# Last group of a four-group transformer kernel: norms four and five, the feed-forward and the second attention's projections by halves of two batches

## What is computed

```
h = tok(x, ids)                          # embeddings, norm, gate
h = h + attn0(norm(h))                   # first attention, causal sums
h = h + ffn0(norm(h))                    # routed attention or mix, then:
#   n2 = norm(h') * g2 + b2
#   ffn = gelu(n2 @ W1 + bf1) @ W2 + bf2      192 -> 768 -> 192
h = h + attn1(norm(h))                   # 12 heads of 16: q, k, v, softmax, sum
h = h + experts(norm(h))                 # top 2 of 8 experts, 192 -> 768 -> 192
norm(x) = (x - mean) / sqrt(var + 1e-5)
```

## Time and profile before

| What | Before |
|---|---|
| Median of 3 runs | 883.57 us (882.9 to 883.79) |
| The profiled execution | 883.04 us, of it 881.2 us span |
| PE busy | 726.0 us (82%), 5500 records |
| DVE busy | 519.7 us (59%) |
| ACT busy | 301.4 us (34%) |
| POOL busy | 242.8 us (28%) |
| Chain that ended last | PE 59%, DVE 21%, issue 6%, ACT 5%, POOL 4%, DMA 3% |

### The profile page before, as it was taken

The page is one execution under the profiler, slowest core; times in us unless marked ns, Lnnn a source line. Parts: engine busy times, 40 slices in busy tenths (PEclk is TensorE's granted clock), DMA queues, the critical chain, the costliest instruction groups (busy, mean ns, idle before and its releaser), DMA issues.

```text
span 881.2 us, 15579 instructions
## 1 busy us (share of the span) xinstructions
PE 726.0 (82%) x5500; PEld 549.1 (62%) x5501; DVE 519.7 (59%) x1752; ACT 301.4 (34%) x688; POOL 242.8 (28%) x300
## 2 busy tenths in 40 slices
PE   0888777989678998868898977959767999999993
PEld 0546465566457565646666655745456988998892
DVE  7558757874678884668877466791344553333330
ACT  0033232624333263434244334313233423333330
POOL 5332200460013245001444200231001453333332
PEclk9999989999988999998899996798897999999997
DMA  7950000000000000000121000029001233222220
GB/s 248 412 244 2 0 1 1 19 8 1 1 1 32 24 19 7 1 2 1 37 37 8 1 2 2 5 94 361 27 1 28 42 73 46 36 37 38 36 35 8
DMA packets 29894, 43.63 MB, mean 50 GB/s; under 512 B 5355, under 2 KB 24597, under 8 KB 29830
## 3 DMA queue, kind: packets, MB, share of 16 engines
q1 hardware_dynamic: 19250, 30.87, 10.2%
q0 software_dynamic: 8752, 9.07, 6.4%
q10 hardware_dynamic: 1828, 2.84, 0.9%
HBM read 21.36 MB, written 22.09 MB: 49 GB/s over the span
## 4 chain that ended last, share of the span: by engine, by line
PE 59%; DVE 21%; issue 6%; ACT 5%; POOL 4%; DMA 3%; ACTq 1%; SPq 1%; DVEq 0%; POOLq 0%
PE qc L1829 26%; PE qa L1829 25%; PE qc L1832 4%; PE qa L1832 4%; DVE mx L1424 2%; DMA out<-qk_T 2%; DVE st L1036 1%; POOL arena_w L435 1%; DMA mu_row<-in_mu 1%; ACT big L791 1%; DVE qk_T L1430 1%; DVE arena_b L1376 1%; ACTq L627 1%; DVE arena_e L1250 1%; DVE xb L1053 1%
## 5 line engine op out<-in xcount | busy, mean ns | idle before, releaser
L1829 PE MATMUL qc<-arena_w,big 128*128 x468 | 82.8, 327 | 1.4 <-DVE qk_T L1808 1.4
L1829 PEld LDWEIGHTS qc<-arena_w,big 128*128 128x128 f32 x468 | 75.1, 190 | 2.1 <-issue 2.0
L1829 PE MATMUL qa<-arena_b 128*128 128x128 f32 (+2 forms) x688 | 73.6, 289 | 3.0 <-DVE att L1440 2.1
L1829 PEld LDWEIGHTS qa<-arena_b 128*128 128x128 f32 (+2 forms) x688 | 64.9, 192 | 11.7 <-issue 2.8
L1829 PE MATMUL qa<-arena_e,nT 128*128 128x192 f32 (+2 forms) x256 | 70.0, 430 | 1.1 <-DVE ga L1320 0.7
L1002 ACT ACTIVATE big<-qa,arena_b 128x128 f32<-128x128 f32 x156 | 43.0, 374 | 75.8 <-PE qc L1829 68.7
L597 POOL DMA_INDIRECT out<-qk_T x39 | 61.0, 1565 | 20.5 <-issue 10.5
L1797 DVE COPY arena_b<-qc 128x256 f32<-128x256 f32 x39 | 16.6, 426 | 84.1 <-PE qc L1832 84.1
L1829 PEld LDWEIGHTS qa<-arena_e,nT 128*128 128x128 f32 x256 | 47.4, 200 | 23.0 <-issue 12.9
L471 POOL TENSOR_TENSOR rs_a<-rs_a,minus_half 128x8 f32<-128x8 f32 x4 | 6.6, 1644 | 175.6 <-DVE rs_a L1287 175.6
L475 POOL TENSOR_TENSOR rs_b<-rs_b,minus_half 128x4 f32<-128x4 f32 x12 | 12.5, 1041 | 152.2 <-DVE rs_b L1049 152.2
(11 more groups left out here) (366 smaller groups left out, 1576.5 us busy)
## 6 DMA issues: line engine op xcount, KB each, us to landing
slots<-xk SPq DMA_DIRECT2D x1, 13192.0 KB, 43.1
arena_e<-in_w SPq DMA_DIRECT2D x8, 579.0 KB, 7.7
arena_w<-in_w SPq DMA_DIRECT2D x8, 576.0 KB, 9.4
qk_T<-slots SPq DMA_DIRECT2D x39, 97.0 KB, 1.9
out<-hb SPq DMA_DIRECT2D x16, 96.0 KB
arena_e<-in_w_l SPq DMA_DIRECT2D x1, 804.0 KB
arena_e<-in_W ACTq DMA_DIRECT2D x1, 768.0 KB
out<-qk_T POOLq DMA_INDIRECT x39, 3.5
```

What stands on the lines that cost most here:

```text
L1829: return nc.tensor.matmul(o, l, r, start=start, stop=stop)
```

## The change

It touches the last group alone; the joint stages keep their code.

- ln4: the statistics, the small operations and the root are made for batches 0 and 1, then for batches 2 and 3 (`half_stats`, `half_apply`, `root_half`). The last group's second `selected_in` moves behind the first half's statistics on DVE.
- Feed-forward: each of the 6 up products becomes two products of 256 tokens; those of the first half wait for the first half of `xT` only. The 6 blocks lie in six banks (PD, PA, PB) instead of taking turns in four. `down_half` waits for the gelus of its own half.
- ln5 by halves in the same way, the first half ahead of `ffn_out` of the second.
- q and k products by halves of 256 tokens in six banks (PA, PB, PC), `v1_half` for two batches behind each half.
- ACT's and POOL's lists follow the same order.

```
+            def root_half(name, n, hf):
+                w(NG - 1, name, n)
+                pool.tensor_tensor(rs_b[:, 1, 2 * hf:2 * hf + 2], rs_b[:, 0, 2 * hf:2 * hf + 2], minus_half[:, 0:2], ALU.pow)\
+                    .then_inc(s["rstd_b"], 1)
...
             def back(tb):
-                root_back(tb, "ln4")
+                root_half("ln4", 9, 0)
+                root_half("ln4", 18, 1)
                 residual(tb, 0)
                 residual(tb, 1)
                 residual(tb, 2)
                 residual(tb, 3)
-                root_back(tb, "ln5")
-                root_back(tb, "ln6")
+                root_half("ln5", 9, 0)
+                root_half("ln5", 20, 1)
+                root_last()
...
+            def gelu_half(tb, j, hf):
+                w(tb, "up", FJ * hf + j + 1)
+                A(hid[:, j, two(hf)], (PD, PA, PB)[j // 2][:, j % 2, two(hf)], ACT.Gelu, bias=bf1c[:, j:j + 1])\
+                    .then_inc(*done("gelu"))
+
+            def qk1_evac_half(tb, n, hf):
+                w(tb, "qk1", 6 * hf + n + 1)
+                A(q1k1[:, n % 2, n // 2, two(hf)], (PA, PB, PC)[n // 2][:, n % 2, two(hf)], ACT.Copy).then_inc(*done("qk1_e"))
...
                 n4T_evac(tb, 0)
                 n4T_evac(tb, 1)
-                ffn_gelu(tb, 0)
...
+                for hf in range(2):
+                    for j in range(FJ):
+                        gelu_half(tb, j, hf)
                 x5T_evac(tb, 0)
+                qk1_evac_half(tb, 0, 0)
+                qk1_evac_half(tb, 1, 0)
+                qk1_evac_half(tb, 2, 0)
+                qk1_evac_half(tb, 3, 0)
                 x5T_evac(tb, 1)
...
+                qk1_evac_half(tb, 4, 0)
+                qk1_evac_half(tb, 5, 0)
                 v1_evac(tb, 0)
+                for n in range(6):
+                    qk1_evac_half(tb, n, 1)
                 v1_evac(tb, 1)
...
             def back(tb):
-                ln4_stats(tb)
-                ln4_apply(tb)
+                ln4_half(tb, 0)
+                selected_in(tb, 1)
+                ln4_half(tb, 1)
+                ln4_half_apply(tb, 0)
+                ln4_half_apply(tb, 1)
                 ffn_out(tb, 0)
+                ln5_half(tb, 0)
+                ln5_half_apply(tb, 0)
                 ffn_out(tb, 1)
-                ln5_stats(tb)
-                ln5_apply(tb)
+                ln5_half(tb, 1)
+                ln5_half_apply(tb, 1)
...
+            def up_half(tb, j, hf):
+                w(tb, "n2T", hf + 1)
+                if j == 4:
+                    w(tb, "hin", 2 * G)
+                if hf:
+                    w(tb, "gelu", j + 1)
+                inc(both((PD, PA, PB)[j // 2][:, j % 2, two(hf)], lambda k: w_up[:, k, j * 128:(j + 1) * 128],
+                         lambda k: xT[:, k, two(hf)]), "up")
+
+            def down_half(tb, b):
+                w(tb, "gelu", FJ * (b // 2 + 1))
...
+            def qk1_half(tb, n, hf):
+                w(tb, "x5T_e", hf + 1)
+                if hf:
+                    w(tb, "qk1_e", n + 1)
+                elif n >= 4:
+                    w(tb, "h_ffn", 2 * (n - 3))
...
             def logits(tb, b, wide=False):
                 lag = 2 if wide else 1
                 if b == 0:
-                    w(tb, "qk1_e", 6)
+                    w(tb, "qk1_e", 12 if wide else 6)
                     w(tb, "v1", 2)
```

More of the change, by code:

```diff
@@ L330, in tok, with two @@
             return slice(b * 128, b * 128 + 128)
+        def two(hf):
+            return slice(hf * 256, hf * 256 + 256)
         def bc(ap, axis, n):
@@ L1449, in ln6_apply @@
                 dve.wait_ge(s["keep"], AHEAD + tb * PER["keep"])
-                dve.wait_ge(s["rstd_b"], root_b(tb, 2) + 1)
+                dve.wait_ge(s["rstd_b"], root_b(tb, 2) + (3 if tb == NG - 1 else 1))
                 norm_apply("ln6", hb, x6, rs_b, mv_b)
@@ L2037, in n4_T @@
                 for b in (2 * hf, 2 * hf + 1):
-                    w(tb, "ln4", 11 + b + 1)
+                    w(tb, "ln4", (18 if tb == NG - 1 else 11) + b + 1)
                     for c in range(C):
@@ L2054, in ffn_down, with v1_half @@
                 inc(i, "down")
+            def up_half(tb, j, hf):
[8 more added lines that the diff above has]
+                w(tb, "gelu", FJ * (b // 2 + 1))
+                for j in range(FJ):
+                    i = mm(psl(PC, b, D), hid[:, j, tok(b)], w_down[:, j, :], j == 0, j == FJ - 1)
+                inc(i, "down")
+            def qk1_half(tb, n, hf):
[4 more added lines that the diff above has]
+                    w(tb, "h_ffn", 2 * (n - 3))
+                j, wt = n // 2, (w_1q, w_1k)[n % 2]
+                inc(both((PA, PB, PC)[j][:, n % 2, two(hf)], lambda k: wt[:, k, 4 * j:4 * j + 4, :].rearrange("p h d -> p (h d)"),
+                         lambda k: xT[:, k, two(hf)]), "qk1")
+            def v1_half(tb, hf):
+                w(tb, "x5T_e", hf + 1)
+                for b in (2 * hf, 2 * hf + 1):
+                    inc(both(psl(PD, b, H * (HD + 1)), lambda c: xT[:, c, tok(b)],
+                             lambda c: w_1v[:, c, :, :].rearrange("p h d -> p (h d)")), "v1p")
             def x5_T(tb, hf):
                 for b in (2 * hf, 2 * hf + 1):
-                    w(tb, "ln5", 11 + b + 1)
+                    w(tb, "ln5", (9 + b + 1 if hf == 0 else 18 + b + 1) if tb == NG - 1 else 11 + b + 1)
                     for c in range(C):
@@ L2346, in back @@
                 n4_T(tb, 0)
+                up_half(tb, 0, 0)
+                up_half(tb, 1, 0)
                 n4_T(tb, 1)
[L2348 to L2356, removed]
-                ffn_down(tb, 3)
+                up_half(tb, 2, 0)
+                up_half(tb, 3, 0)
+                up_half(tb, 4, 0)
+                up_half(tb, 5, 0)
+                for j in range(FJ):
+                    up_half(tb, j, 1)
+                for b in range(G):
+                    down_half(tb, b)
                 x5_T(tb, 0)
+                qk1_half(tb, 0, 0)
+                qk1_half(tb, 1, 0)
+                qk1_half(tb, 2, 0)
+                qk1_half(tb, 3, 0)
                 x5_T(tb, 1)
-                qk1(tb, 0)
-                qk1(tb, 1)
-                qk1(tb, 2)
-                qk1(tb, 3)
-                qk1(tb, 4)
-                qk1(tb, 5)
-                v1_rows(tb, 0)
-                v1_rows(tb, 1)
+                qk1_half(tb, 4, 0)
+                qk1_half(tb, 5, 0)
+                v1_half(tb, 0)
+                for n in range(6):
+                    qk1_half(tb, n, 1)
+                v1_half(tb, 1)
                 logits(tb, 0, True)
```

50 lines of the change are left out of this document (38 added, 12 removed).

## The result

The change takes the kernel to 879.12 us (median of 6 runs, 870.22 to 880.45); the kernel before, run beside it, takes 882.82 (881.65 to 883.79). The ratio is 0.9944, 95% interval 0.9917 to 0.9971: faster by 3.7 us, 3 us short of the forecast of 876.0 and inside its range. That fall is where to look: the stages that the change touches did slightly better than forecast, and something behind them got slower.

The account below looks back on a forecast made before the run. Bound: one chain through the last group's back stage, where PE's waits for ln4 and ln5 also slow its clock. Gains 1.2 + 6.4 = 7.6 took the profiled 883.04 to 875.4, median 876.0 us; range 873.0 to 879.5.

Parts of the forecast that it names:

- First part, ln4 and up: ln4 to down products: halves start the up products 1.65 us earlier, partly lost to slow clock; gain 1.2 (1.0 to 1.8).
- lock rule: Named with a first part of 1.0 and a late first half for the upper 877.5; not defined in the text given.
- The up phase's other waits: Up phase: last-gelu wait of 0.76 us goes, first gelu has 1 us of slack, POOL's later residuals cost nothing.
- Second part, ln5 and q, k, v: Down products to first logits: first half's norm hidden, 8.05 against 8.08 us; 15.9 instead of 22.3, gain 6.4.
- Half-width records: Up, q and k products: 0.22 us per 256-column record, bounds 0.217 and 0.23; 48 records take 10.56 us.
- The rival of narrow products that pay for their loads: The 96 new records: loads not hidden, 0.38 us each, 15.4 more, 891.4 us; chance 0.03.
- What comes behind: After the logits: expert weights land at about 619, over 20 us cover their reader, and the gain reaches the end.
- the clock is less kind: Attention or pause before q and k: more slow clock costs 3 us, 879.0; one slow stretch alone 877.5; chance 0.18.
- a chance to gain: Slow stretch from 667.03 to 677.28, around the first expert products: at full clock 2.9 us saved, 873.1; chance 0.14.
- The prediction's own sign of being wrong: Behind the changed stages: the logits come early, at about 634.3, and the expert tiles do not.

Follow-up runs that it names:

- ln4 filled: Changed kernel with eight unread products in attention gaps, plus five more while PE waits for ln4: 869.55 us, ratio 0.9838 to the kernel before.
- the four profiles: Changed kernel unchanged (879.12 and 886.5 us), with four unread products ahead of the first logits (880.67), and with two behind them (884.63).
- the shift: Changed kernel with four unread products ahead of the last group's first logits, putting its attention off: 880.67 us.
- the filled kernels: Changed kernel and kernel before, each with eight unread products in the last group's attention gaps: 878.27 against 889.96 us, then 878.18 against 889.94.
- the changed kernel with two fillers: Changed kernel with only two unread 512-column products, behind the first batch's logits: 884.63 us, ratio 0.989 to the kernel before.
- the second set: Later runs together: changed kernel unchanged 886.5 us, kernel before 893.4, both with eight unread products 878.18 and 889.94, changed with two 884.63.

## Why the prediction was right in its place and short in its size

**First part, ln4 and up: right, more than taken.** Predicted were up products 7.2 us behind the selected rows, down products 13.0 to 13.8 behind the up products, and a gain of 1.2 (1.0 to 1.8). Measured: 6.49, 13.87, gain 2.36 - 0.70 = 1.66. Three terms made the start earlier. The half chains were shorter: from the first half's rows to the second's (590.87) it is 1.93 us, not 2.12, and both variances are done 3.96 behind the start, not 4.24. Most of that is the selected rows, 0.53 for a pair and not 0.68; the seven small operations take 0.84 on two columns where they took 0.86 on four. The root takes 0.70 to 0.76, not 1.02. And the first applies were not slowed: 0.66 for two beside the root, at the lower end of the two values the step kept open. The pair began before the second root (592.98, 0.76 long) and ended while it ran, the second apply inside it, at undisturbed length (0.67 at ln5 with POOL idle). The prediction's upper value of 877.5 takes in a "lock rule": no run shows such a term, and what the runs showed in its place are these 0.66 us with the root running beside them. Beside POOL's additions the next pair did double (1.31), as the earlier trace rows had shown. The other half of the step was right as well: the earlier start cost more slow clock, 2.8 us of it (13.87 against 11.1), and with ln4 filled the phase takes 10.90, so that there was no more to get in it.

**The up phase's other waits: right.** No wait for the last gelu, none for the first, whose table is loaded by 602.41: the first two gelus end at 603.27, and PE comes to the second half's first block at 604.12; the residuals end at 598.6 and delay nobody.

**Second part, ln5 and q, k, v: right.** The first half's normed rows are ready 7.62 us behind the first down product (predicted 8.05 of 8.08): the narrow root took 0.71, and sum, statistics and small operations took less than their 2.10. The cover was 7.80 us and not 8.08 (the transposes start at 617.10), so 0.2 us were left, and PE did not wait. q follows 1.12 behind the down products (1.2), the clock stays at 1.00, and the second half's transposes run at 621.94, 1.1 us after their rows are ready (0.8). From the last down product to the logits 15.64 (15.9). Gain 6.75, predicted 6.4.

**Half-width records: right.** Sixteen of them take 3.45 us in the chain, 0.216 each, at the lower bound of 0.217. The rival of narrow products that pay for their loads is out.

**What comes behind: right for transfers and experts, wrong for the attention.** The weights have landed by about 620, and windows over the expert loop show PE as full as before (19.80 of 20.00 at 720 to 740). The term that failed is in the rival "the clock is less kind": "a second and third of these, with 3.08 busy each, cost at most 1.5 each", with a price of 3 and a chance of 0.18, and against it "PE's own pattern stays". I had read the 3.42 us of the earlier trace rows as the length of a slow stretch. It was the length of one, and the second line of the same rows showed another of 10.25 us, with 2.98 of its first 3.42 busy, which I took for a chance to gain and not for a warning. At a granted clock of 0.50 this attention keeps PE busy for 2.2 to 2.9 us of each 3.4 up to its last wait, and in none of the four profiles did the clock return before the expert products. ("Busy half of the time" was low as well: it is 17.95 of 30.40 us, 0.59.)

The price of that case was 6.05 us in the profile (8.07 more of PE's busy time, 2 of it in gaps), double the 3 taken, and by times and clocks it was the common case, in five of six runs. So the rival that I gave 0.18 is what came, at 879.12 beside its 879.0, and it came that near by luck: the price was 3 too low, against it the stages were worth 0.8 more, the expert loop lost one slow stretch, 1.75, and 0.66 arose ahead of the change. The prediction's own sign of being wrong, logits that come early and expert tiles that do not, was there in part: 9.1 us and 3.0.

**What stays open.** Why the clock stays low through the changed kernel's attention and not through the other's is not shown: the shift moved the fall and did not remove it, and the change itself is not ruled out as the cause. Neither is it known why the kernel before differs by 10 us between sets; clock and pauses in the expert tiles both have a part in it.

## What to carry to other kernels

When a change moves a stage in which PE is busy for only part of the time (here 17.95 of 30.40 us), price it twice, with that stage at either clock: a slow stretch seen once, and short, says little about how long the next one is (here 3.42 us before the change and 37.5 after it). A saving that brings no clock with it should be measured with idle gaps filled in both kernels: here the filled kernels differ by 11.7 and 11.8 us, the unfilled ones by 3.7 and 6.9. Then look whether the clock was the same in the stages without fillers, for here it was not, and 8.4 us is what the stages themselves show. And where PE must wait in any case, a few products that nobody reads can be the cheapest lines in the kernel: eight of them gave 8.3 us, five more 3.1.

## What the runs showed of the hardware

- The granted clock of the changed kernel stays at 0.50 for 37.5 us at one go, while PE is busy for most of the time (for instance 2.94 of 3.40 us). PE's waits in that stretch are for DVE and ACT, 0.35 to 0.80 us each and one of 2.13. The traces give this clock as a share of full speed; none shows it in GHz, as the prediction and two of the expectations put it.
- With the first gap filled, the clock fell with no wait of PE over 0.96 us since the first logits (the changed kernel with two fillers).
- One execution in six of the changed kernel took 870.22 us beside 878.32 to 880.45, at a mean clock of 0.932 beside 0.917 to 0.923; none of the ten of the second set did so. That it escaped the slow attention is likely but not shown, since it was not profiled.
- A power of -1/2 on POOL over two columns takes 0.70 to 0.76 us, over four 1.02, and the applies of DVE beside it took no longer (0.33 each); beside POOL's additions of 192 columns they took double (0.65 each).
